# State-space stage: who adds the two halves of the softplus, GpSimd in four instructions or VectorE in two

## What is computed

```python
dBu = xc @ x_proj_w + x_proj_b
delta_s, B, u = jnp.split(dBu, [d_state, 2 * d_state], axis=-1)
delta = jax.nn.softplus(delta_s @ dt_proj_w + dt_proj_b)
A = -jnp.arange(1, d_state + 1)
deltaA = jnp.exp(delta[..., None] * A)
deltaB_u = delta[..., None] * B[:, :, None, :] * u[..., None]
# over the 512 times of a row:  h = deltaA * h + deltaB_u ;  y = h.sum(-1)
```

## Time and profile before

| | |
|---|---|
| time, median of 3 runs | 3105.36 us (3100.03 to 3111.36) |
| span of the profiled execution, first to last instruction | 3008.1 us |
| median less span | 97.3 us |
| PE busy | 2783.3 us (93%) |
| DVE busy | 2329.8 us (77%) |
| POOL busy | 2187.8 us (73%) |
| ACT busy | 1803.2 us (60%) |

### The profile page before, as it was taken

How to read it: one execution, slowest core, us unless ns; L and a number is a source line. 1 busy time by engine, 2 the same in 40 slices (tenths; PEclk the granted TensorE clock), 3 DMA queues, 4 the chain that set the end, 5 groups by cost and what they waited for, 6 DMA issues and landing times. The chain is left out here.

```text
span 3008.1 us, 54043 instructions
## 1 busy us (share of the span) xinstructions
PE 2783.3 (93%) x16944; PEld 2226.0 (74%) x16944; DVE 2329.8 (77%) x4122; ACT 1803.2 (60%) x3430; POOL 2187.8 (73%) x1437
## 2 busy tenths in 40 slices
PE   6999989989989899899985899999899997999998
PEld 3566656566656566666664799999899997999998
DVE  4899998989989999899998667575567776666665
ACT  4766776667657766677663545454456664454553
POOL 4888998898989889989987665665335557565654
PEclk8999999999999999999998899999999997999999
DMA  6222221121112211221125454544333334454542
GB/s 169 74 103 73 87 73 40 62 88 71 46 59 87 74 44 59 88 73 44 52 80 205 128 117 115 118 118 115 68 103 116 116 130 130 113 125 112 126 111 36
DMA packets 192665, 281.66 MB, mean 94 GB/s; under 512 B 35943, under 2 KB 164622, under 8 KB 184264
## 3 DMA queue, kind: packets, MB, share of 16 engines
q1 hardware_dynamic: 157128, 236.31, 23.7%
q0 software_dynamic: 35328, 42.76, 7.9%
HBM read 197.28 MB, written 94.72 MB: 97 GB/s over the span
## 5 line engine op out<-in xcount | busy, mean ns | idle before, releaser
L550 POOL TENSOR_TENSOR dbu<-du,bb 128x1024 f32<-128x1024 f32 x512 | 1196.3, 2361 | 30.0 <-DVE hs L703 26.7
L703 DVE TENSOR_TENSOR_SCAN hs<-da,dbu 128x1024 f32<-128x1024 f32 x512 | 1150.7, 2279 | 81.0 <-ACT da L638 39.8
L638 ACT ACTIVATE da<-delta 128x512 f32<-128x512 f32 x1024 | 566.4, 594 | 239.0 <-DVE hs L703 228.6
L808 PEld LDWEIGHTS yT<-ident,hs 128*128 128x128 f32 x4096 | 482.8, 146 | 151.6 <-issue 85.8
L808 PE MATMUL yT<-ident,hs 128*128 128x128 f32 x4096 | 542.5, 282 | 19.7 <-DVE hs L703 19.7
L1371 POOL TENSOR_TENSOR ffn_w_lo<-ffn_w,ffn_w_hi 128x512 fp32r<-128x512 f32 x240 | 323.8, 1377 | 93.8 <-ACT ffn_w_hi L1366 93.8
L1451 PE MATMUL ffn_ybank<-ffn_w_hi,ffn_hT_hi 128*128 128x256 f32 x1280 | 367.2, 287 | 0.6 <-DVE ffn_hT_lo L1439 0.6
L1453 PE MATMUL ffn_ybank<-ffn_w_hi,ffn_hT_lo 128*128 128x256 f32 x1280 | 360.6, 282 | 0.0
L1452 PE MATMUL ffn_ybank<-ffn_w_lo,ffn_hT_hi 128*128 128x256 f32 x1280 | 359.8, 281 | 0.0
L1417 PE MATMUL ffn_hbank<-ffn_rowsT_hi,ffn_w_hi 128*128 128x320 f32 x1024 | 339.0, 331 | 3.3 <-POOL ffn_w_lo L1371 3.3
L1428 ACT ACTIVATE ffn_hT_hi<-ffn_hbank,ffn_b 128x320 fp32r<-128x320 f32 x512 | 269.2, 526 | 113.0 <-PE ffn_hbank L1419 113.0
(11 more groups left out here) (257 smaller groups left out, 4962.2 us busy)
## 6 DMA issues: line engine op xcount, KB each, us to landing
bb<-b_rows SPq DMA_DIRECT2D x64, 1024.0 KB, 4.6
ffn_w<-L_ffn_W SPq DMA_DIRECT2D x60, 1024.0 KB, 5.8
slots<-empty SPq DMA_DIRECT2D x40, 530.0 KB, 9.1
empty<-slots SPq DMA_DIRECT2D x16, 662.5 KB, 4.8
ffn_rows<-slots SPq DMA_DIRECT2D x16, 662.5 KB, 4.9
xt<-L_attn_a_x SPq DMA_DIRECT2D x16, 512.0 KB, 4.0
x<-L_attn_a_x SPq DMA_DIRECT2D x16, 512.0 KB, 4.0
x_after_mamba<-x SPq DMA_DIRECT2D x16, 512.0 KB, 2.9
```

Of the source, the lines that this page charges most:

```text
L550: pool.tensor_tensor(dbu[:, s % DEEP], du[:, dt, :].unsqueeze(1).to_broadcast([P, SN, T]), bb[:, q * SN:(q + 1) * SN, :], ALU.mult).then_i ...
L638: ins = act.activation(da[:, s % 2, i, :], delta[:, par, dt, :], ACT.Exp, scale=-float(q * SN + i + 1))
L703: dve.tensor_tensor_scan(flat[0], flat[1], flat[2], 0.0, ALU.mult, ALU.add).then_inc(scanned.sem, 1)
L808: mm = pe.matmul(yT[:, j * P:(j + 1) * P], hs[:, s % DEEP, i, j * P:(j + 1) * P], k.ident[:], start=False, stop=(q == QS - 1 and i == SN - ...
```

## The change

`softplus` leaves GpSimd and becomes a function of VectorE. It adds a range of blocks in one instruction: block 0 alone (128x512), and blocks 1 to 3 together (128x1536). Block 0 stands after the scan of step 25, directly ahead of `step_input` of block 0, which moves with it from step 24 to step 25. Blocks 1 to 3 stand at step 28, after the gate `silu_z`. GpSimd's four additions go, and with them its wait for `log_part`. Nothing else is moved.

```diff
-        def softplus(pool, row, par, m):
-            pool.wait_ge(log_done.sem, log_done.at(row, 1))
-            pool.tensor_tensor(delta[:, par, m, :], delta[:, par, m, :], tail_of_xc[:, m, :],
-                               ALU.add).then_inc(delta_ready.sem, 1)
...
+        def softplus(dve, row, par, first, blocks):
+            dve.wait_ge(log_done.sem, log_done.at(row, 1))
+            dve.tensor_tensor(delta[:, par, first:first + blocks, :], delta[:, par, first:first + blocks, :],
+                              tail_of_xc[:, first:first + blocks, :], ALU.add).then_inc(delta_ready.sem, blocks)
...
-                        if s == 26 and has_first(turn):
-                            softplus(pool, turn, par, 0)
-                        if s == 30 and has_first(turn):
-                            softplus(pool, turn, par, 1)
-                            softplus(pool, turn, par, 2)
-                        if s == 31 and has_first(turn):
-                            softplus(pool, turn, par, 3)
...
-                        if s == 24 and first:
+                        if s == 25 and first:
+                            softplus(dve, turn, par, 0, 1)
                             step_input(dve, turn, turn, par, 0)
                         if s == 28 and main:
                             silu_z(dve, turn, 2)
+                        if s == 28 and first:
+                            softplus(dve, turn, par, 1, ND - 1)
```

## The result

| | before | changed |
|---|---|---|
| median of 4 runs each | 3102.7 us | 3175.1 us |
| lowest to highest | 3093.7 to 3111.4 | 3166.5 to 3188.1 |
| ratio, 95% interval | 1 | 1.0245 [1.0213, 1.0277] |
| DVE, POOL busy in the profiled execution | 2329.8, 2187.8 us | 2405.9, 2124.3 us |
| a turn without a jump, with one | 98.3, 101.4 us | 104.0, 106.7 us |

The forecast was 3178 us in 3140 to 3200, slower with a chance of 0.87. The two medians lie 72 us apart; the ratio makes 76 us of it. For an account by parts I take three lengths from each trace: the pitch of the turns (from one `r_below` to the next, from turn 2 to turn 15: eight without a jump and five with one), the start of the first `r_below`, in turn 2, and the end of the state-space stage, where the experts' first matmul runs.

The account below looks back on a forecast made before the run. VectorE was taken to lead at the turn's end, all others following. 3.5 us in 15 turns (52.5 us) plus 2.2 us in 9 turns (20 us) made 72.5 us on 3105.4: 3178 us, range 3140 to 3200.

Parts of the forecast that it names:

- 0.9 and 0.2 us for `du` and `r_below`: Per turn: `du` of block 0 behind the scan of step 25 adds 0.9 us, `r_below` held at step 23 adds 0.2.
- 0.6 plus 0.3 of hold and 1.65, with 0.15 off for TensorE: Per turn: block 0's sum 0.6 us plus 0.3 waiting, big sum 1.65, less 0.15 for TensorE's wait overtaken at step 28.
- row estimate of 1.73 us: Length of the sum of blocks 1 to 3 at step 28, from 682 ns plus 1.03 ns for each of 1024 more elements.
- it waits 0.3 us: Step 25: `dbu` of step 28 outlasts the scan by 0.2 to 0.3 us, so block 0's sum waits 0.3 us.
- The hold at step 28: Big sum waits 2.2 us for `dbu` of the next turn's step 0, in 9 turns of 15: 20 us; chance 0.45.
- the margin of 0.15 us: Step 28: the big sum comes up 0.15 us after `dbu` of the next turn's step 0 starts.
- the 1.87 us of ScalarE: ScalarE's time at a jump back with nothing to wait for; turns with a jump were expected to have VectorE first.
- held in every turn: Rival: the jump is hidden, 15 x 5.7 = 85.5 us, 3191 us; chance 0.12, a third of it with the longer wait.
- the longer wait: Block 0's sum at step 25 also meets the start of a `dbu`: 2.0 us more per turn, 3221 us.
- the 2 us that I had left open: Turn 0: big sum and `du` of block 1 replace a 2.55 us wait; may gain or lose 2 us, left at zero.
- The 97.3 us outside the span: Time taken to lie outside the 3008.1 us span and to stay untouched by the change.
- Its wait at step 28: TensorE's 0.32 us wait is overtaken because the scan comes later; half taken, -0.15 us a turn.

Follow-up runs that it names:

- kernel without sums: Both VectorE sums left out of the changed kernel, which only waits for the logarithm and counts blocks as ready: 3114.5 us, 1.0021 to before.
- big sum at step 29: Sum of blocks 1 to 3 moved from step 28 to directly behind the scan of step 29, against the changed kernel: 3154.7 us, 1.0144 to before.
- second trace of before: The kernel before, without an edit, profiled once more on a second chip: 3012.7 us.
- block 0 in the gap: Against block 0 alone on VectorE: its sum and `du` at step 24, GpSimd waiting for that `du` before `dbu` of step 27: 3030.0 us, 1.0067 to before.

## Why the prediction was right, point by point

**Direction and mechanism: right.** VectorE leads at the end of the turn, all other engines follow, and what it gets is paid in full. The kernel without sums shows it from the other side: a GpSimd that is free of its additions gives nothing.

**The own work: right.** In a turn without a jump, the steps gave 0.9 and 0.2 us for `du` and `r_below`, measured 0.98 together (no sums, less before). For the two sums the steps gave 0.6 plus 0.3 of hold and 1.65, with 0.15 off for TensorE, 2.4; measured 2.6 (big sum at step 29, less no sums). From 128x512 to 128x1536 the row estimate of 1.73 us was met exactly.

**The sum of block 0 was not held.** Step "it waits 0.3 us" failed. The scan of step 25 ended as the `dbu` did, the sum took 0.67 us and the `dbu` behind it was held. In its place stands a term that I had not seen: `du` needs this sum, and waits 0.20 us for it, an instruction that reads what the one directly ahead of it wrote.

**The hold at step 28: size right, count wrong.** It measured 2.12 us a turn against the 2.2 forecast (changed, less big sum at step 29), and the margin of 0.15 us was met (0.13 to 0.16). But I had it in 9 turns of 15, since GpSimd's jump would let VectorE be first in the others. It came in every turn. GpSimd's three `dbu` take 6.99 to 7.00 us in the turns with a jump and 6.98 to 7.01 in those without: whatever its jump costs was hidden behind the `dbu` in work. The step that failed was to carry the 1.87 us of ScalarE, an engine with nothing under way, over to one with work queued. By its mechanism the outcome is thus the rival "held in every turn", without the longer wait; the price of that rival, 85.5 us, was too high.

**Why the sum came out at 76 all the same.** Two kinds of error offset each other, and that 3178 lies so near 3175 is in part luck. The hold in six more turns adds 13 us, to 85.5. Against it stands the account of the trace: 71.8 us over the 13 turns from turn 2 to 15 (eight of +5.7, five of +5.2), 3.7 us ahead of the first of these (2.4 against the second trace of before) and 4.3 us behind the last, 79.8 in all.

The 3.7 us come from turns 0 and 1. Turn 0 costs 1.2 us, inside the 2 us that I had left open: the first scan starts at 58.38 in place of 57.19. Turn 1 has the 5.7 us too, but two things gave 3.4 back at its start. One is a wait of 1.81 us marked as issue, now 0.44; it is 3.25 in the second trace of before, so it may be chance. The other is a cast of 32x256, with one input, of before and of the changed kernel:

```profile
62.30 2.32 DVE L681 CAST b_out<-x 32x256 bf16<-32x256 f32 x1
```

```profile
63.80 0.28 DVE L677 CAST b_out<-x 32x256 bf16<-32x256 f32 x1
```

Before, GpSimd had a `dbu` in work until 64.48, and the cast ended at 64.62; in the changed kernel it isn't held. The second trace of before has it at 2.33 us, the kernel without sums at 0.28. So the new order of the two engines' work made one hold of 2.0 us go away, which I hadn't looked for.

Turns with a jump grew by half a microsecond less than the others, and by their means the hold is worth 1.1 us there and not 2.1 (106.65 less 105.53). The five turns one by one show 2.5, 0.2, 0.7, 2.4 and -0.1 us, so the mean says little. In the second, for example, VectorE has all of the 2.1 us until its waits for `da` after the jump; one of those is 2.98 us in the kernel with the sum at step 29 and 1.17 in the changed one. What makes these waits differ no experiment took apart.

**The 97.3 us outside the span: wrong, without effect.** It is 1.8 us. The difference was added to the median and not to the span, so the step had no hold on the result; had the attention stage reacted to the change, it would have misled.

**TensorE.** Its wait at step 28 is gone, as forecast, and a much longer one has come up: with the sum ahead of the last scans, TensorE has nothing to do for 6 us in the turn shown above, before 1.2. The 24 matmuls behind it, of before and of the changed kernel:

```profile
1042.68 0.66 PE L816 MATMUL ring<-ident,ysb 128*128 128x128 f32 x4 [1.21 <-ACT uD L628]
...
1043.42 2.82 PE L808 MATMUL yT<-ident,hs 128*128 128x128 f32 x24
```

```profile
1096.27 1.12 PE L817 MATMUL ring<-ident,ysb 128*128 128x128 f32 x4 [6.03 <-ACT uD L624]
...
1097.49 4.70 PE L809 MATMUL yT<-ident,hs 128*128 128x128 f32 x24
```

They take 4.70 us against 2.82. The windows around these matmuls, of before and of the changed kernel, with the columns of the earlier trace rows:

```profile
1043.40:1046.20 2.80, 2.80 (x31) 2.60 (x27) 2.64 (x4) 0.61 (x1) 2.80 (x2) 1.00 0.37 149
```

```profile
1097.40:1102.20 4.80, 4.80 (x34) 4.80 (x32) 4.26 (x16) 0.94 (x2) 0.00 (x0) 0.59 0.00 2
```

The granted clock was 1.00 after 1.21 us of idle time, and 0.59, between the levels of 1.2 and 2.4 GHz, after 6.03. VectorE's scan after them waits 3.07 us for them, where the earlier trace rows has 3.05 for ScalarE, so little of it seems to reach the path here; no experiment tested that.

None of the versions beats the kernel before. The nearest in which VectorE makes a sum is that with block 0 in the gap, 0.7% slower.

## What to carry to other kernels

Ask first which engine leads, and count work moved onto it at full length, whatever the engine that loses it had to do. Where two engines can shut each other out, lay their instructions on one time line and look who comes up first: 0.15 us decided over 25 us here, and exchanging two neighbours or moving an addition behind the scan for which the other engine is waiting took most of the hold back. An overhead seen on an idle engine says nothing of one with queued work, and a lead that looks like idle time should be kept until a run shows that it is worth nothing: without it the late engine can hold a tiny instruction of the leading one.

## What the runs showed of the hardware that I had not expected

- The hold works both ways and is decided by who comes up first: the big sum takes 3.84 us when a `dbu` is in work, and three `dbu` take 8.50 us in place of 7.00 when the sum is first.
- It takes tiny instructions as well: a subtraction of 128x32 went from 0.17 to 1.5 us. Copies and casts with one input are held too: one of 128x4 took 0.58 to 1.50 us in place of 0.17, one of 32x256 2.32 in place of 0.28. A reduction of 128x1536 values (1.75 us) and a multiplication with one input in PSUM (0.69 us at most) were not held at all.
- At a loop's jump ScalarE stands 1.87 us; on GpSimd, with `dbu` queued, three of them across the jump take 6.99 to 7.00 us, and 6.98 to 7.01 where there is none.
- An unchanged kernel took 3010 us on one chip and 3105 on another, 3% apart. In the kernels that were traced, the attention stage took 292 us on the one and 356 to 378 on the other.
